# Row maxima of two heads in one VectorE instruction, a fourth score bank, and fewer, longer runs of value products

## The reference

```python
pos = jnp.arange(S)
idx = jnp.clip(pos[None, :] - pos[:, None], -MAX_REL, MAX_REL) + MAX_REL
rk2 = rel_k[idx]
rv2 = rel_v[idx]
attn1 = jnp.einsum('bhqd,bhkd->bhqk', q, k)
attn2 = jnp.einsum('bhqd,qkd->bhqk', q, rk2)
attn = jax.nn.softmax((attn1 + attn2) / scale, axis=-1)
w1 = jnp.einsum('bhqk,bhkd->bhqd', attn, v)
w2 = jnp.einsum('bhqk,qkd->bhqd', attn, rv2)
x = (w1 + w2).transpose(0, 2, 1, 3).reshape(B, S, E)
out = x @ Wo.T + bo
```

## Time and profile before

| | |
|---|---|
| median of 3 runs | 1425.4 us (1424.68 to 1428.78) |
| the profiled execution, its own time | 1427.91 us |
| its span, first to last instruction | 1426.0 us |
| TensorE matmul busy | 1281.4 us (90%) |
| VectorE busy | 948.1 us (66%) |
| ScalarE busy | 758.8 us (53%) |
| GpSimd busy | 550.8 us (39%) |
| granted TensorE clock, mean | 0.960 |

### The profile page before, as it was taken

The page is one execution under the profiler, slowest core; times in us unless marked ns, Lnnn a source line. Parts: engine busy times, 40 slices in busy tenths (PEclk is TensorE's granted clock), DMA queues, the critical chain, the costliest instruction groups (busy, mean ns, idle before and its releaser), DMA issues. The chain is left out here.

```text
span 1426.0 us, 67609 instructions
## 1 busy us (share of the span) xinstructions
PE 1281.4 (90%) x30680; PEld 941.6 (66%) x30688; DVE 948.1 (66%) x1844; ACT 758.8 (53%) x1413; POOL 550.8 (39%) x983
## 2 busy tenths in 40 slices
PE   4377669999999999999999999999999999889998
PEld 2244337777777777777777776777777777656665
DVE  6499777776766766766767667667767676055554
ACT  4276526565655655655656556556556566422222
POOL 4376533543435343435334353434344343022221
PEclk9689859999999999999999999999999999989999
DMA  4445420202020202112020202021120200122321
GB/s 138 114 168 183 155 57 8 53 23 63 9 64 20 53 20 55 25 48 53 20 63 13 64 20 53 21 54 30 43 55 21 64 9 9 41 60 67 89 67 45
DMA packets 101541, 79.08 MB, mean 55 GB/s; under 512 B 13256, under 2 KB 97032, under 8 KB 101256
## 3 DMA queue, kind: packets, MB, share of 16 engines
q1 hardware_dynamic: 101256, 74.77, 19.1%
HBM read 45.90 MB, written 27.26 MB: 51 GB/s over the span
## 5 line engine op out<-in xcount | busy, mean ns | idle before, releaser
L1039 DVE TENSOR_REDUCE b_mx<-b_a 128x1 f32<-128x512 f32 x1024 | 658.7, 685 | 239.2 <-PE b_a L806 233.8
L1000 ACT ACTIVATE b_p<-b_s 128x512 f32<-128x512 f32 x1024 | 569.8, 595 | 417.5 <-PE b_s L847 332.8
L897 PE MATMUL b_pv<-b_p,vg 128*16 128x128 f32 x8192 | 286.8, 275 | 0.0
L770 POOL TENSOR_TENSOR qd<-q,one 48x512 bf16<-48x512 bf16 x256 | 266.1, 1040 | 30.1 <-POOLq L286 5.3
L747 POOL TENSOR_TENSOR b_np<-vg,one 128x16 bf16<-128x16 f32 x192 | 39.1, 264 | 581.1 <-DVE b_mx L1039 570.3
L847 PE MATMUL b_s<-qd,z 112*128 112x32 bf16 (+1 forms) x6016 | 248.9, 189 | 2.8 <-issue 2.8
L806 PE MATMUL b_a<-k,q 48*128 48x512 bf16 x1024 | 203.6, 394 | 28.2 <-DVE b_mx L1039 12.6
L847 PEld LDWEIGHTS b_s<-qd,z 112*128 112x128 bf16 x6016 | 206.0, 99 | 15.2 <-issue 5.3
L897 PEld LDWEIGHTS b_pv<-b_p,vg 128*16 128x16 f32 x8192 | 196.3, 96 | 21.1 <-issue 0.2
L832 PE MATMUL b_s<-q,k 54*128 54x64 bf16 (+3 forms) x4608 | 187.8, 201 | 6.8 <-issue 3.3
L832 PEld LDWEIGHTS b_s<-q,k 54*128 54x128 bf16 (+1 forms) x4608 | 126.2, 95 | 92.2 <-PE b_s L832 29.2
(11 more groups left out here) (125 smaller groups left out, 1312.7 us busy)
## 6 DMA issues: line engine op xcount, KB each, us to landing
x<-in_x SPq DMA_DIRECT2D x32, 256.0 KB, 3.1
scratch_qop<-a_parts SPq DMA_DIRECT2D x16, 384.0 KB, 2.5
scratch_kop<-a_parts SPq DMA_DIRECT2D x16, 384.0 KB, 3.1
k<-scratch_kop SPq DMA_DIRECT2D x32, 192.0 KB
q<-scratch_qop SPq DMA_DIRECT2D x32, 192.0 KB
scratch_v<-a_vr SPq DMA_DIRECT2D x16, 256.0 KB, 3.2
k<-scratch_kop SPq DMA_DIRECT2D x32, 128.0 KB
q<-scratch_qop SPq DMA_DIRECT2D x32, 128.0 KB
```

What stands on the lines that cost most here:

```text
L770: nc.gpsimd.tensor_tensor(dst, src, one, ALU.mult).then_inc(s["qd_ready"], 1)
L897: nc.tensor.matmul(PV[32 * a:32 * a + V16, g * P:(g + 1) * P], v[:, 0 if t <= i else 1, t, h, :], PR[at.c % 2][:, t, h, :], start=(t == 0 ...
L1000: nc.scalar.activation(out, src, ACT.Exp, scale=SCALE).then_inc(s["p_ready"], 1)
L1039: nc.vector.tensor_reduce(MX[v.c % 2][:, h:h + 1], PA[(n + hp) % NBANK][:, :], AX_X, ALU.max, negate=True).then_inc(s["a_used"], 1)
```

## The change

There are now four score banks, made as one tile `SR`, and `b_a` is one tile of two banks for one pair of heads. `row_max` is one instruction over both heads. A pair may start only when the pair before it has been read entirely (`pairs_done`); for the first 8 pairs of the program the score banks serve as a second tile. With four score banks the scores of step c wait for the exponentials of step c-2. The pairs no longer stand one at each step: a table `SPOTS` puts each of the 8 at the start or at the end of a step, by i. The value products of the last key block move from step 0 to step 1, ahead of the relative values; those of key blocks 0 and 1 both follow step 5; key block 2 stays after step 7.

```diff
-NBANK = 3
+NBANK = 4
...
-    SC = [m.ps(f"b_s{n}", [P, S]) for n in range(NBANK)]
-    PA = [m.ps(f"b_a{n}", [P, S]) for n in range(NBANK)]
+    SR = m.ps("b_s", [P, NBANK, S])
+    SC = [SR[:, n, :] for n in range(NBANK)]
+    PA = m.ps("b_a", [P, HP, S])
...
+    START, END = 0, 1
+    SPOTS = (((0, START), (1, START), (1, END), (2, START), (3, START), (4, START), (5, END), (6, START)),
+             ((0, START), (1, END), (2, START), (2, END), (3, START), (4, START), (5, END), (6, START)),
+             ((0, START), (2, START), (3, START), (4, START), (5, START), (5, END), (6, START), (7, END)),
+             ((0, START), (2, START), (3, START), (4, START), (5, END), (6, START), (7, START), (7, END)))
...
+    def pair_banks(n):
+
+        return SR[:, 0:HP, :] if n < HH and n % 2 else PA[:, :, :]
+
+    def pairs_done(n):
+
+        return n - 1 if n <= HH else n
...
-                if n + HP > NBANK:
-                    pe.wait_ge(s["a_used"], n + HP - NBANK)
+                if pairs_done(n) > 0:
+                    pe.wait_ge(s["a_used"], pairs_done(n))
...
                 both_halves(at, c, (0, 1), True).then_inc(s["half"], 1)
-                row_pairs_ahead(at, c)
+                row_pairs_ahead(at, c, START)
                 pe.wait_ge(s["half"], halves_done(at, c))
                 both_halves(at, c, (1, 0), False)
                 relative_scores(at, c).then_inc(s["s_ready"], 2)
+                row_pairs_ahead(at, c, END)
...
-                        if c == 0:
+                        if c == 1:
                             value_products(before, T - 1)
-                        if c == 1:
...
-                    if c == 4:
+                    if c == 5:
                         value_products(at, 0)
-                    if c in (5, 6):
-                        value_products(at, 1, range(H // NQ4)[2 * (c - 5):2 * (c - 4)])
+                        value_products(at, 1)
                     if c == 7:
                         value_products(at, 2)
...
-                for hp in range(HP):
-                    h = 2 * hh + hp
-                    dve.wait_ge(s["a_ready"], n + hp + 1)
-                    if h == 0 and v.since(2):
-                        dve.wait_ge(s["guard"], v.count(NGD, 1 - 2 * NGD))
-                    nc.vector.tensor_reduce(MX[v.c % 2][:, h:h + 1], PA[(n + hp) % NBANK][:, :], AX_X, ALU.max,
-                                            negate=True).then_inc(s["a_used"], 1)
+                dve.wait_ge(s["a_ready"], HP * (n + 1))
+                if hh == 0 and v.since(2):
+                    dve.wait_ge(s["guard"], v.count(NGD, 1 - 2 * NGD))
+                nc.vector.tensor_reduce(MX[v.c % 2][:, 2 * hh:2 * hh + HP], pair_banks(n), AX_X, ALU.max,
+                                        negate=True).then_inc(s["a_used"], 1)
```

More of the change, by code:

```diff
@@ L633, in stage_attend, with pairs_beside @@
     EARLY = HH // 2
-    order = [(0, hh) for hh in range(HH)] + [(1, hh) for hh in range(EARLY)]
[L635 to L639, removed]
+    START, END = 0, 1
[3 more added lines that the diff above has]
+             ((0, START), (2, START), (3, START), (4, START), (5, END), (6, START), (7, START), (7, END)))
+    def pairs_beside(u, c, side):
+        left = [(1, EARLY + c)] * (u == 0 and side == START and c < HH - EARLY)
+        return left + [(u + LEAD, hh) for hh, spot in enumerate(SPOTS[u % T]) if spot == (c, side) and u + LEAD < U]
+    order = [(0, hh) for hh in range(HH)] + [(1, hh) for hh in range(EARLY)]
+    for u in range(U):
+        for c in range(SUB):
+            order += pairs_beside(u, c, START) + pairs_beside(u, c, END)
     place = {pair: n for n, pair in enumerate(order)}
-    def pairs_beside(at, c):
-        u = at.count()
-        return [(1, EARLY + c)] * (u == 0 and c < HH - EARLY) + [(u + LEAD, c)] * (u + LEAD < U)
+    def pair_banks(n):
+        return SR[:, 0:HP, :] if n < HH and n % 2 else PA[:, :, :]
+    def pairs_done(n):
+        return n - 1 if n <= HH else n
     def window(t, i):
@@ L735, in link @@
                     pool.wait_ge(s["guard"], at.count(NGD, n))
-                pool.wait_ge(s["a_used"], HP * (place[at.count(), HH - 1] + 1))
+                pool.wait_ge(s["a_used"], place[at.count(), HH - 1] + 1)
                 if i == 0:
@@ L797, in row_pair, with row_pairs_ahead @@
             def row_pair(v, hh):
-                p, i, n = (v.c // T) % 2, v.c % T, HP * place[v.count(), hh]
+                p, i, n = (v.c // T) % 2, v.c % T, place[v.count(), hh]
                 if i == 0 and hh == 0:
                     pe.wait_ge(kq_in[p], (v.even(T) + 1) * (16 * NKQ))
-                if n + HP > NBANK:
-                    pe.wait_ge(s["a_used"], n + HP - NBANK)
+                if pairs_done(n) > 0:
+                    pe.wait_ge(s["a_used"], pairs_done(n))
                 for hp in range(HP):
                     r = slice(HALF * hp, HALF * hp + OPR)
-                    nc.tensor.matmul(PA[(n + hp) % NBANK][:, :], Q[p][r, hh, hp, i * P:(i + 1) * P], K[p][r, hh, :],
+                    nc.tensor.matmul(pair_banks(n)[:, hp, :], Q[p][r, hh, hp, i * P:(i + 1) * P], K[p][r, hh, :],
                                      start=True, stop=True).then_inc(s["a_ready"], 1)
-            def row_pairs_ahead(at, c):
-                for u, hh in pairs_beside(at, c):
+            def row_pairs_ahead(at, c, side):
+                for u, hh in pairs_beside(at.count(), c, side):
                     row_pair(at.plus(u - at.count()), hh)
@@ L869, in scores @@
                         if n == 0:
-                            row_pairs_ahead(at, c)
+                            row_pairs_ahead(at, c, START)
                         diagonal_scores(at, c, n)
                         relative_scores(at, c, n).then_inc(s["s_ready"], 1)
+                    row_pairs_ahead(at, c, END)
                     return
-                if at.since(1) or c >= 1:
+                if at.since(1) or 2 * c + 1 >= NBANK:
                     pe.wait_ge(s["p_ready"], freed(at, 2 * c + 1))
                 if not window(t, i):
-                    row_pairs_ahead(at, c)
+                    row_pairs_ahead(at, c, START)
                     both_halves(at, c, (0, 1), True).then_inc(s["s_ready"], 2)
+                    row_pairs_ahead(at, c, END)
                     return
                 both_halves(at, c, (0, 1), True).then_inc(s["half"], 1)
-                row_pairs_ahead(at, c)
+                row_pairs_ahead(at, c, START)
                 pe.wait_ge(s["half"], halves_done(at, c))
@@ L1032, in row_max @@
             def row_max(v, hh):
[L1033 to L1040 removed]
+                n = place[v.count(), hh]
+                dve.wait_ge(s["a_ready"], HP * (n + 1))
[3 more added lines that the diff above has]
+                                        negate=True).then_inc(s["a_used"], 1)
             def keep_values(at):
@@ L1066, in unit @@
                 for c in range(SUB):
-                    for u, hh in pairs_beside(at, c):
-                        row_max(at.plus(u - at.count()), hh)
+                    for side in (START, END):
+                        for u, hh in pairs_beside(at.count(), c, side):
+                            row_max(at.plus(u - at.count()), hh)
                     if before.exists():
```

## The result

The changed kernel takes 1470.6 us (median of 4, 1468.0 to 1473.8) beside 1426.1 us for the kernel before on the same chip: a ratio of 1.031, 95% interval 1.028 to 1.034. The prediction was 1465, with a range of 1436 to 1490. The profiled execution took 1473.8 us, 45.9 more than the one of before.

A forecast was written before the change was run, and what follows sets the result against it. TensorE, 90% busy, was taken as the likely bound: its own sequence plus short waits. Terms 47 - 6 - 17 + 13 + 3 = +40 on the profiled 1427.9 gave 1468, as median 1465 us, range 1436 to 1490.

The forecast's parts named there:

- Term 1: Attention: TensorE waits for VectorE to finish reading the single pair tile, 3.05 us a sequence over 15.5 sequences, +47 us.
- 0.37 was forecast: END of step 7 to START of step 0 (i = 2 to 3 and 3 to 0): wait for VectorE of 0.37 us, twice.
- 0.39 was: START of step 3 to START of step 4, i = 0 and i = 2: wait for VectorE of 0.39 us, twice.
- the 1.06: START of step 4 to END of step 5, i = 0: one wait for VectorE of 1.06 us a sequence.
- the 0.5 of small ones: Waits for VectorE around step 2 of i = 1 (0.2 and 0.2) and at step 4 of i = 3 (0.1).
- Term 2: TensorE's waits for ScalarE: a fourth score bank removes 21 us, new waits of 0.95 a sequence add 15; -6 us.
- Term 3: Changes of TensorE layout over the attention fall from 1353 to 1203, 150 at 0.115 us each: -17 us.
- term 4: 62 row pairs no longer between the halves of a beside step cost their 0.21 us in the open: +13 us.
- the switch that had no row: L847 to L806, relative scores to an END pair: taken at 0.115 us; if free, term 3 would be -44.
- Term 5: Start of the stage: first 8 pairs gain 1 us from two tiles, some 8 later ones lose 3 to 5; +3 us.
- The faster case: Rival: a run's boundary costs 0.33 us and the END switch nothing, so 192 saved runs give about 1420 us; chance 0.11.
- The small loss: Rival: the new switch costs nothing and the two-bank reduction takes 1.10 us; 1427 to 1440, say 1435; chance 0.14.

The follow-up runs named there:

- the control: Kernel before with each maximum over the first 256 of its 512 columns: 1418.3 us; the same edit in the changed kernel took 1409.4 us.
- e5: Kernel before with the row pair of each beside step moved from between the two groups of 8 matmuls to behind the relative scores: 1489.7 us.
- e3: Kernel before with only the value products placed as in the change, three score banks and three row banks kept: 1490.3 us.
- e7: Changed kernel with the value products placed as before; four score banks, pair tile and table of pairs kept: 1525.7 us.
- the two kernels with short maxima: Changed kernel and kernel before, each with maxima over the first 256 of 512 columns: 1409.4 and 1418.3 us.
- e6: Kernel before, its banks and pairs kept, with value products merged only where three score banks allow it, by query block: 1423.7 us.
- e10: Kernel before, three banks of each kind and one maximum per head, with its own table of pair places and value products: 1399.1 us.
- e12: Kernel before with the table of pair places of e10 but its own value products: 1410.7 us.

## Why the prediction was right

It was right in sign, size and mechanism: 1465 forecast, 1470.6 measured; by the profiled executions +40 forecast and +45.9 measured.

- **Term 1, VectorE waits, +47.** Right in kind, too small. Against the control, the tile costs (1470.6 - 1426.1) + (1418.3 - 1409.4) = 53 us, where terms 1 and 5 said 50. The reduction is 1.223 in place of 1.20, and the cycle 1.75 to 1.82 in place of 1.70: VectorE starts 0.47 behind the pair and, where the pair has to change the layout as well, TensorE goes 0.11 behind its end and not 0.05 to 0.07. The single wait of 1.06 came out to the hundredth in the profile's own figure. Start to start, in the traced sequence (811 to 875 us), the waits are 0.48 where 0.37 was forecast, twice, 0.51 where 0.39 was, twice, 1.11 for the 1.06, and 0.11, 0.29 and 0.33 for the 0.5 of small ones: 3.8 us and not 3.05, 12 us more over 15.5 sequences. That the 45.9 us by which the profile's group of waits grew look like the 47 is chance, for that group holds the start and leaves out what stands under other names.
- **Why the sum was right all the same.** A sequence grew by 2.4 us, which is just the 37 us of terms 1 to 4. Some 12 us that term 1 lacked were made up elsewhere: about 4 in term 2, and about 8 in stretches of up to 2 us in which TensorE stood still with no cause in the profile ("issue" of its matmuls between 230 and 1200 us, 18 us before and 11 now), which no term speaks of. That part is luck.
- **Term 2, ScalarE waits, -6.** In the right direction. The weight loads' waits fell from 53.6 in 160 to 31.9 in 63, but much of what is left is the tile's wait under ScalarE's name, as at step 4 of i = 0, so the view does not give the term cleanly. The new waits, put at 0.95 a sequence, are some 0.66 in the traced one: 0.52 at step 1 of i = 2, put at 0.7 (0.49 of idle below), and 0.05 to 0.09 at two others. That is about 4 us less:

```profile
848.12 0.23 PEld L845 LDWEIGHTS b_s<-q,k 51*128 51x128 bf16 x8 [0.49 <-ACT b_p L1014]
```

- **Term 3, layout changes, -17, and term 4, lost cover, +13.** Both prices were tested by e5 at once: 64 by the counted order, 64 measured. So the switch that had no row is paid (L847 to a pair, 0.35). Each price alone was not varied. The counts of the prediction, 1353 and 1203, are those of the traces; it was the expectations of e3 and e7 that priced a run as two changes. Together with term 2 they are the 9 us between the two kernels with short maxima, where 10 were forecast. The Trainium skill, TensorEngine Tiling (Array Packing), Key Properties, says that a change of tiling mode drains TensorE. The trace agrees for the new switch too, in that it costs 0.11.
- **Term 5, the start, +3.** 38.5 us to the second guard transpose, 36.3 before: +2.2. The signs of its parts were right too: to the first guard transpose, where the pairs have two tiles, it is 12.4 us in place of 14.3, and the loss comes after it.
- **The rivals.** The faster case hung on a run's boundary of 0.33 and a free END switch. e5 shows the switch at 0.11, and at 0.33 the runs put back in e7 would alone cost 63 us, where 55 were measured with 40 us more of waits for VectorE. The small loss hung on a reduction of 1.10; it is 1.22.

The misses were in small edits outside the forecast: e6 by 5 to 9 us, e10 and e12 by 12.

## What to carry to other kernels

Count the distance between two uses of a single buffer at the place where it is shortest, not on average: VectorE was at 62%, and a tile whose cycle (write, read, release) of 1.8 us fitted 8 times into a unit of some 17 us still cost 50 us. A long gap elsewhere does not give back what a short one costs, since all that stands behind the waiting pair in TensorE's order waits too. Merging two instructions into one saves their fixed part but releases both buffers late: with two tiles that was a gain (1.9 us over the first 8 pairs), with one it was a wait. Count changes of layout in the order itself; "so many runs fewer, two changes each" was 14 us wrong in e3 and e7. And when banks are moved from one use to another, try first what a better order gives with the banks as they are: here it gave 28 us.

## What the runs showed of the hardware

Each change between matmuls that take half the rows, the whole array or a strip of columns costs 0.09 to 0.12 us in these traces, in whichever direction, and also after matmuls of only 16 and 32 columns (L847 to a pair: 0.35 against 0.24 to 0.25 ahead of the whole layout). A maximum over 2 x 256, 2 x 384 and 2 x 512 columns in one instruction took 0.689, 0.955 and 1.223 us, so 0.27 for each 256 columns more, and over one bank of 512 it took 0.685, as long as over 2 x 256.

The mean granted clock differed between the kernels' profiles, 0.957 to 0.966, and also between runs of one kernel: of 15 runs of the kernel before, the fastest (1420.5 us) had 0.964 and the slowest (1435.6) 0.957. The difference of 0.007 is 20 us at 1.2 GHz and up to 10 us of time. So differences of a few us between single profiles say little here, and even medians can carry some of it.
